# A gated graph network on one core: where VectorE reads the third gate, and where four smaller pieces of its work stand

## What is computed

```
for _ in range(5):
    s_in, s_out = state @ in_W.T + in_b, state @ out_W.T + out_b
    a_in, a_out = A @ s_in, A.T @ s_out
    a = concat([a_in, a_out, state])
    r, z = sigmoid(a @ r_W.T + r_b), sigmoid(a @ z_W.T + z_b)
    h = tanh(concat([a_in, a_out, r * state]) @ h_W.T + h_b)
    state = (1 - z) * state + z * h
out = tanh(state @ o1_W.T + o1_b) @ o2_W.T + o2_b
return layernorm(x + out)
```

## Time and profile before

| what | us |
|---|---|
| median of 3 runs (lowest, highest) | 656.99 (656.04, 657.47) |
| the profiled execution, its own time | 657.65 |
| its span in the trace | 655.9 |
| PE busy | 638.1 |
| DVE busy | 524.4 |
| ACT busy | 418.2 |
| POOL busy | 68.1 |

### The profile page before, as it was taken

The page is one execution under the profiler, slowest core; times in us unless marked ns, Lnnn a source line. Parts: engine busy times, 40 slices in busy tenths (PEclk is TensorE's granted clock), DMA queues, the critical chain, the costliest instruction groups (busy, mean ns, idle before and its releaser), DMA issues. The chain is left out here.

```text
span 655.9 us, 8678 instructions
## 1 busy us (share of the span) xinstructions
PE 638.1 (97%) x2860; PEld 525.3 (80%) x2860; DVE 524.4 (80%) x833; ACT 418.2 (64%) x562; POOL 68.1 (10%) x61
## 2 busy tenths in 40 slices
PE   8999999999999999999999999999999999999993
PEld 7888888887888788788888877888887888887883
DVE  4996889799578739987896998887689888746886
ACT  2774645478357726895665688575758966674645
POOL 0092025200500720000000000000000000000012
PEclk9999999999999999999999999999999999999998
DMA  8999657213200270324034223403342250213003
GB/s 290 332 360 239 169 179 195 42 46 49 101 1 32 58 196 37 67 63 161 33 131 66 92 63 66 160 32 128 58 134 55 42 193 1 96 65 129 1 0 132
DMA packets 111609, 70.40 MB, mean 107 GB/s; under 512 B 89424, under 2 KB 95696, under 8 KB 110544
## 3 DMA queue, kind: packets, MB, share of 16 engines
q1 hardware_dynamic: 103056, 68.84, 35.1%
q10 hardware_dynamic: 8512, 1.05, 1.1%
HBM read 47.85 MB, written 19.40 MB: 103 GB/s over the span
## 5 line engine op out<-in xcount | busy, mean ns | idle before, releaser
L1158 ACT ACTIVATE work<-work,bias 128x512 f32<-128x512 f32 x120 | 86.0, 723 | 125.2 <-DVE work L1679 124.6
L1679 DVE SCALAR_TENSOR_TENSOR work<-degree,deg_w,bank 128x512 f32<-128x512 uint16 x120 | 88.4, 744 | 28.1 <-PE bank L703 27.3
L1017 ACT ACTIVATE ring<-a 128x1024 fp32r<-128x1024 uint8 (+1 forms) x91 | 91.7, 1048 | 6.3 <-PE bank L822 3.1
L701 PE MATMUL bank<-u_c,fold 128*128 128x512 f32 x240 | 94.1, 392 | 1.6 <-DVE work L1679 1.5
L702 PE MATMUL bank<-u_c,fold 128*128 128x512 f32 x240 | 93.4, 389 | 0.0
L703 PE MATMUL bank<-u_c,fold 128*128 128x512 f32 x240 | 93.4, 389 | 0.0
L822 PE MATMUL bank<-ring,rows 128*128 128x512 f32 x384 | 90.8, 390 | 0.3 <-DVE ring L1452 0.3
L714 PE MATMUL bank<-ring,rows 128*128 128x512 f32 x384 | 88.6, 389 | 0.2 <-issue 0.2
L1050 ACT ACTIVATE ring<-sums,minus 128x1024 fp32r<-128x1024 uint8 x72 | 80.3, 1139 | 7.5 <-PE bank L822 6.5
L822 PEld LDWEIGHTS bank<-ring,rows 128*128 128x128 f32 x384 | 71.7, 188 | 16.5 <-DVE ring L1452 1.0
L714 PEld LDWEIGHTS bank<-ring,rows 128*128 128x128 f32 x384 | 72.0, 188 | 15.5 <-issue 0.6
(11 more groups left out here) (168 smaller groups left out, 1110.9 us busy)
## 6 DMA issues: line engine op xcount, KB each, us to landing
sums<-sums_dram SPq DMA_DIRECT2D x12, 768.0 KB, 5.0
stage<-in_adj_dram SPq DMA_DIRECT2D x15, 512.0 KB, 8.6
sums<-in_adj_dram SPq DMA_DIRECT2D x13, 512.0 KB, 6.4
turned_dram<-work SPq DMA_DIRECT2D x12, 512.0 KB, 2.6
rows<-turned_dram SPq DMA_DIRECT2D x192, 32.0 KB, 2.0
sums_dram<-sums SPq DMA_DIRECT2D x4, 768.0 KB, 3.5
l_dram<-rs_c SPq DMA_DIRECT2D x3, 1024.0 KB, 3.9
rs_c<-l_dram SPq DMA_DIRECT2D x3, 1024.0 KB, 4.9
```

The costliest lines, as they stand in the source:

```text
L701: nc.tensor.matmul(out_, wh, vh, start=first, stop=False)
L1017: nc.scalar.activation(out_, in_, ACT.Copy).then_inc(s, 1)
L1158: nc.scalar.activation(gates[:, g, e, :], gates[:, g, e, :], ACT.Tanh if g == H else ACT.Sigmoid, bias=bias[:, g, e:e + 1]).then_inc(gate_ ...
L1679: nc.vector.scalar_tensor_tensor(out=gates[:, g, e, :], in0=degree[:, c * CW:(c + 1) * CW], scalar=deg_w[:, g, e:e + 1], in1=g_bank[s % 3] ...
```

## The change

Four edits, of order and of one wait:

1. In chunk 3 of every step, and chunk 1 of steps 1 to 4, DVE reads gate 2 directly behind gate 1. Before, it did so behind r * state for both halves, with the transposes and the first low part between. ACT's and PE's lists stay.
2. At the end of chunk 3 of step 0 and of chunk 1 of step 1 the state's split is taken out on ACT and DVE. It stands inside step 1's `half_aggregate` now, on ACT behind the casts 13 and 15, on DVE behind four symmetry tests.
3. In `aggregate_pair`, first side, the low parts of chunk 1's rows go from before the third and fourth DVE casts to behind them.
4. POOL starts the third portion of byte sums when mix W5 of step 1's second side is done, not when chunk 1's update is.

```diff
@@ POOL
             sum_blocks(1, range(6))
-            pool.wait_ge(state_new, S_TWO + 2 * TWO)
+            pool.wait_ge(mixed, mixed_at(1, 1, W5))
             pool.wait_ge(sums_kept[0], 16)
             pool.wait_ge(pair_used, used_at(1, 0, P3, 1))
             sum_blocks(2, range(6))
@@ ACT, gate_chunk_two
                 gate(t, c, 3)
-                if not ending:
+                if not ending and not half(t + (c == NC - 1)):
                     for e in range(DB):
                         split_state(*((t, 2) if c == 1 else (t + 1, 0)), e)
@@ ACT, half_aggregate
                 for k in range(12, 16):
                     cast(t, side, k)
+                    if k % 2 == 1:
+                        split_state(t, 2 * side, k // 2 - 6)
@@ DVE, gate_chunk
                     update(t, c - 1, first_gate=lambda: gate(t, c, 0))
                     next_pair(0)
                     gate(t, c, 1)
+                    gate(t, c, 2)
                     rs(t, c, 0)
                     final(0)
...
-                gate(t, c, 2)
+                if not (c == NC - 1 or c == 1 and not first):
+                    gate(t, c, 2)
                 rs_low(t, c, 1)
                 final(2)
...
-                if c == NC - 1 and not last or c == 1 and not first:
+                if (c == NC - 1 and not last or c == 1 and not first) and not half(t + (c == NC - 1)):
                     for e in range(DB):
                         split_state(*((t, 2) if c == 1 else (t + 1, 0)), e)
@@ DVE, half_aggregate
                 for _ in range(4):
                     test()
+                for e in range(DB):
+                    split_state(t, 2 * side, e)
                 if side == 0:
                     row_low(t, 3, 0)
@@ DVE, aggregate_pair
                 if side == 0:
                     row_low(t, L1, 0)
-                    for h in range(2):
-                        row_low(t, 1, h)
...
                 cast(t, side, 3)
+                if side == 0:
+                    for h in range(2):
+                        row_low(t, 1, h)
```

## The result

The changed kernel takes 659.73 us (median of 6 runs, 659.57 to 660.59), the kernel before in the same series 657.08 (6 runs, 656.04 to 657.47). The ratio is 1.0045, interval 1.0032 to 1.0058: slower by 3.0 us by the ratio, 2.7 by the two medians. The prediction said 659.9, 2.9 more.

What follows compares the result with a forecast made beforehand. PE, busy 638.1 of 655.9 us, was taken to bound the kernel, only its waits being winnable. Terms +0.1 + 1.5 + 1.15 - 0.55 - 1.2 - 0.57 + 2.5 = +2.9 on 656.99 gave 659.9 us; own range 658.4 to 661.2, 8-in-10 range 656.2 to 661.2.

Steps and rivals of the forecast that it cites:

- Third read, chunk 3: Chunk 3 of steps 0 to 3: PE's stall for gate 2's read is exchanged for one at rs_c's low part, +0.1 us.
- What that pushes: Starts of steps 2, 3 and 4: work behind the read moves 0.66, ACT's fifth cast is late, +0.5 each, +1.5 us.
- Chunk 1: Third read in chunk 1: late fifth cast costs +0.4 in steps 2 and 3, +0.35 in step 4, 0 in step 1; +1.15.
- Splits of step 1: Into step 1: gate reads and ACT's casts come 0.54 earlier, the two stalls for casts stay, -0.55 us.
- Byte sums: Step 1's second side: DVE's second cast no longer runs beside POOL's sums, PE's 0.95 wait goes, -1.2 us.
- Low parts of the rows: Near 401: casts ahead of chunk 1's low parts release PE sooner, -0.57 us once.
- Last chunk: Last step's chunk 3: DVE waits 4.4 us before the third read, so gate 5 is read later, +2.5 us.
- A: Rival: pushes end in DVE's idle time and only the gains remain, 654.8 us (652.8 if PE also wins stalls); chance 0.12.
- B: Rival: only the hold in the last chunk is covered, 657.4 us; chance 0.13.
- C: Rival: the pushed casts are in time and only the last chunk costs, 657.3 us; chance 0.12.

Runs made afterwards that it cites:

- kernels with late splits: Splits of steps 2 to 4 moved behind the side's first eight casts: in the changed kernel 659.59 us, in it without any third read moved 656.44.
- kernel of chunk 1 alone: Kernel with the three other edits and no third read moved, plus the third read moved in chunk 1 of steps 1 to 4 only: 654.91 us.
- the read alone: Kernel before the change with only the third read (gate 2) moved, none of the other three edits: 663.96 us, ratio 1.0107.
- the first experiment: Changed kernel with only the third read of the last step's chunk 3 put back to its old place: 657.59 us, ratio 1.0015.
- kernels of chunk 3 and chunk 1 alone: Other three edits kept, third read moved only in chunk 3 of steps 0 to 3 (655.66 us), or only in chunk 1 of steps 1 to 4 (654.91).

## Why the prediction was right

**Verdict and time.** 659.9 was said and 659.73 measured, and the stretches of the table follow the terms one by one, none off by more than 0.3. That the sum is so near is partly luck: the last chunk came out at 2.3 by the distances and 2.0 by the ratios for 2.5, chunk 1 of steps 2 to 4 at 1.3 to 1.6 for 1.15, and one ratio alone is good to about 0.6 us. The lower end of the stated own range, 658.4, is 1.5 below the sum where the text names 1.3.

**Third read, chunk 3.** The stall was exchanged for one at rs_c's low part, as said. +0.1 in all was taken. In the kernels with late splits, where the cast is in time, the moved read makes the rs_c matmuls of steps 1 to 3 come 0.06 to 0.11 earlier and those behind them 0.13 to 0.17 later, so 0.2 in all.

**What that pushes.** +0.5 each was said for steps 2 to 4; 0.55 to 0.58 is what the stretches give once the 0.13 to 0.17 that stays with late splits is taken off.

**Chunk 1.** +1.15 was said, 0.34 + 0.38 + 0.61 = 1.33 in the table, 1.4 by the ratios. The margin at rs_c held with 0.11. The cost is made of the small delays described above rather than of one of 0.25. The mis-sized part is step 4: 0.35 said, 0.61 measured. The second side of step 1, which I had at 0, costs 0.13 in the change and 0.17 in the kernel of chunk 1 alone; without edit 2 it is 0.7.

**Splits of step 1.** -0.55 was the net of two effects, -1.20 and +0.66; -0.46 is in the table. Alone, the splits shorten the stretch by 1.20, and the moved read takes 0.70 back. One of the two stalls stayed, at 0.33; that both would stay was wrong.

**Byte sums.** -1.2 was said, -1.12 is in the table with the 0.13 of the read in it, and -1.29 with this edit alone. By the ratio the edit alone is worth 0.7, with an interval of 0.1 to 1.3.

**Low parts of the rows.** -0.57 was said, 0.6 measured alone, and -0.04 in the table, against +0.5 - 0.57. The two were summed as independent, and they are not: in this stretch edit 3 alone gives -0.64, the read alone +0.08 and all edits -0.04. The pushed PE no longer met the late cast of the earlier trace rows, so beside the moved read edit 3 gains 0.1 there, not 0.6, and without edit 3 the push would have cost as little. The sum of the row came out right while its parts did not, which is luck.

**Last chunk.** +2.5 was said, +2.30 on PE, 2.0 by the ratios. The working's residual at 629.95 (14.84 behind the second read) came at 14.73, its fourth gate at 14.19 came at 14.07. From there to gate 5's read it was 3.70 for 3.80.

**The rivals.** A (absorbed pushes) falls with the cast's waits and the 18.43; B with the first experiment, where the last chunk is worth 2.0; C with the kernels of chunk 3 and chunk 1 alone, 2.1 and 1.4. A's gains without its losses exist, but only without the moved read: 653.67, where A had 654.8.

## What to carry to other kernels

An instruction that waits for a producer costs what the producer is still missing, for everything behind it in an in-order queue; before moving a read up, subtract the read's new place from the producer's end (here 0 in chunk 3, 1.6 in chunk 1, 4.3 in the last, where 1.3 was waited before), and look for the hole that it filled where it stood. A stall removed is worth what the next late piece leaves of it: read the margins of the casts, low parts and loads behind it first (the fifth cast's was 0.40 us, the push 0.66). When edits are judged one at a time, look at both the ratio and the trace: one trace is one execution, and a wait in it (0.68 us in the kernel with the splits alone) may be missing in most others.

## What the runs showed of the hardware

DVE operations with two sources in SBUF got longer beside POOL's byte sums, and not only the casts. Four symmetry tests take 5.28 in the changed kernel, where a pair without POOL takes 1.41 in step 2 of the kernel with no third read moved; the two low parts of the state behind them take 3.22 instead of 1.29. An operation that reads a PSUM bank takes its 0.69 beside POOL too (231.69 above). POOL's own additions of byte tiles take 1.42 and 1.48 beside the tests and 1.04 where DVE is idle (at 229.13). So moving the sums cost DVE 4.4 us of its idle time, 8.02 to 3.66, and nothing was waited for there: the term of the byte sums stood with 3.7 us to spare.

Operation by operation the two engines take turns:

```profile
220.32 1.41 DVE L1598 SCALAR_TENSOR_TENSOR stage<-stage,a 128x512 uint32<-128x512 uint32 x1
221.15 1.48 POOL L647 TENSOR_TENSOR sums<-a,byte_two 128x512 uint32<-128x512 uint32 x1
221.77 1.41 DVE L1598 SCALAR_TENSOR_TENSOR stage<-stage,a 128x512 uint32<-128x512 uint32 x1
```

The first POOL addition ends at 221.19, and the DVE test that began at 220.32 at 221.73, 0.54 later; the next POOL addition ends at 222.63, 0.90 behind that, and the next test at 223.18, 0.55 later still. The two low parts end 0.54 and 0.55 behind a POOL addition too, and in the kernel before both casts of 215.50 end 1.08 behind one. So each waits for what is left of the other's operation, and then does its own part. The Trainium skill (SBUF — State Buffer, Who interferes with whom) has it that the loser of the shared port waits the whole instruction out; the trace agrees. A DVE operation is longer by less than one POOL operation (0.7 for a test, about 1.0 for a low part or cast) because the POOL operation is already under way when it begins.

A late operand can cost without any idle time in a row. On the second sides of steps 2 and 3 the changed kernel has no row with an idle time on PE, and yet the stretches are 0.34 and 0.38 longer, by matmuls that start 0.34 or 0.24 apart. The summed waits miss that; distances between fixed matmuls don't.
